# An attention and expert layer on one core: tile 0 is loaded turned, its mean is taken off by products, and its q is made ahead of k and v

## The reference, cut to what matters

```python
def _layernorm(x, axis=-1, eps=1e-05):
    m = jnp.mean(x, axis=axis, keepdims=True)
    v = jnp.var(x, axis=axis, keepdims=True)
    return (x - m) / jnp.sqrt(v + eps)
...
        q = jnp.einsum('bse,ef->bsf', query, Wq)
        k = jnp.einsum('bse,ef->bsf', key, Wk)
        v = jnp.einsum('bse,ef->bsf', value, Wv)
        q = q * cos + _rotate_half(q) * sin
        k = k * cos + _rotate_half(k) * sin
        probs = jax.nn.softmax(jnp.einsum('bhqd,bhkd->bhqk', q, k) * scale, axis=-1)
        ctx = jnp.einsum('bhqk,bhkd->bhqd', probs, v)
        return jnp.einsum('bsf,fe->bse', ctx, Wo)
...
    x = x + xattn(_layernorm(x), ctx_4096, ctx_4096, positions, Wq, Wk, Wv, Wo)
    x = x + ffn(_layernorm(x), A_w, B_w, Wq_w, keys)
```

## Time and profile before

| | before |
|---|---|
| median of 3 runs | 166.45 us (166.23 to 168.49) |
| the profiled execution | 166.19 us |
| its span | 163.6 us |
| outside the span | 2.6 us |
| busy, share of the span | PE 97%, PEld 79%, DVE 83%, ACT 58%, POOL 55% |
| mean granted TensorE clock | 1.000 |
| DMA | 18.45 MB, 113 GB/s on average |
| the chain that ended last | PE 95%, DVE 2%, issue 1% |

### The profile page before, as it was taken

How to read it: one execution, slowest core, us unless ns; L and a number is a source line. 1 busy time by engine, 2 the same in 40 slices (tenths; PEclk the granted TensorE clock), 3 DMA queues, 4 the chain that set the end, 5 groups by cost and what they waited for, 6 DMA issues and landing times.

```text
span 163.6 us, 4199 instructions
## 1 busy us (share of the span) xinstructions
PE 158.4 (97%) x1437; PEld 128.7 (79%) x1437; DVE 135.8 (83%) x394; ACT 95.5 (58%) x215; POOL 89.6 (55%) x115
## 2 busy tenths in 40 slices
PE   6799999999999999999999999999999999999993
PEld 2557886777889787979787987979799986789883
DVE  1979896997998999799888998799886997868562
ACT  3598999899675463933678238832478064414210
POOL 6389999999969944625932098106360305220300
PEclk9999999999999999999999999999999999999999
DMA  5999961403312283434623342133410001000013
GB/s 162 356 411 393 409 221 68 134 31 98 92 48 50 79 251 97 116 112 100 166 85 94 81 105 56 50 98 87 107 62 23 4 0 55 11 6 0 0 64 128
DMA packets 12116, 18.45 MB, mean 113 GB/s; under 512 B 2496, under 2 KB 5056, under 8 KB 11840
## 3 DMA queue, kind: packets, MB, share of 16 engines
q1 hardware_dynamic: 10944, 16.36, 31.7%
q10 hardware_dynamic: 1152, 1.84, 3.7%
HBM read 11.11 MB, written 2.10 MB: 81 GB/s over the span
## 4 chain that ended last, share of the span: by engine, by line
PE 95%; DVE 2%; issue 1%; ACT 0%
PE ps_w L1365 14%; PE ps_w L1370 13%; PE ps_w L1366 12%; PE ps_t L1378 8%; PE ps_w L1358 4%; PE ps_s L1451 4%; PE ps_w L1360 3%; PE ps_w L1359 3%; PE ps_s L1470 3%; PE ps_s L1521 3%; PE ps_t L1521 3%; PE ps_s L1491 2%; PE ps_s L1504 2%; PE ps_t L1370 2%; PE ps_t L1366 2%; PE ps_t L1365 2%
## 5 line engine op out<-in xcount | busy, mean ns | idle before, releaser
L476 POOL TENSOR_TENSOR late<-late,gate 128x512 f32<-128x512 f32 x7 | 7.6, 1087 | 34.3 <-DVE gate L1147 19.3
L707 ACT ACTIVATE eT<-ps_s 128x512 f32<-128x512 f32 x32 | 17.1, 602 | 1.7 <-PE ps_s L1491 0.9
L461 POOL TENSOR_TENSOR oT_lo<-o_n,oT_hi 128x512 fp32r<-128x512 f32 x8 | 10.4, 1296 | 5.3 <-ACT oT_hi L715 5.3
L1365 PE MATMUL ps_w<-am_hi,x2T_hi 128*128 128x288 f32 x44 | 12.6, 308 | 0.0
L1366 PE MATMUL ps_w<-am_lo,x2T_hi 128*128 128x288 f32 x44 | 12.0, 295 | 0.0
L1365 PE MATMUL ps_w<-b_hi,zT_hi 128*128 128x512 f32 (+1 forms) x28 | 11.1, 402 | 0.0
L759 ACT ACTIVATE zT_hi<-ps_t 128x512 fp32r<-128x512 f32 x7 | 4.2, 598 | 11.7 <-PE ps_t L1378 11.7
L1358 PE MATMUL ps_w<-wq_hi,xT_hi 128*128 128x512 f32 x26 | 10.9, 418 | 0.0
L1038 DVE TENSOR_REDUCE ps_s<-ps_s 128x8 f32<-128x512 f32 x16 | 10.6, 688 | 0.3 <-PE ps_s L1451 0.2
L1048 DVE TENSOR_REDUCE ps_s<-ps_s 128x8 f32<-128x512 f32 x16 | 10.4, 691 | 0.5 <-PE ps_s L1470 0.3
L406 POOL TENSOR_TENSOR rstd<-ve,neg_half 128x1 f32<-128x1 f32 x8 | 4.4, 554 | 11.5 <-DVE ve L966 10.2
(11 more groups left out here) (283 smaller groups left out, 551.7 us busy)
## 6 DMA issues: line engine op xcount, KB each, us to landing
x_sb<-x SPq DMA_DIRECT2D x8, 256.0 KB, 6.4
q_stack<-qT_hi SPq DMA_DIRECT2D x32, 64.0 KB, 2.0
cT_in<-cT SPq DMA_DIRECT2D x6, 256.0 KB, 4.1
wq_sb<-wq SPq DMA_DIRECT2D x4, 256.0 KB, 4.4
late<-wo SPq DMA_DIRECT2D x1, 1024.0 KB, 7.2
am_sb<-aT SPq DMA_DIRECT2D x1, 1024.0 KB, 8.9
b_sb<-bT SPq DMA_DIRECT2D x1, 1024.0 KB, 7.3
k_stack<-k_bd_hi SPq DMA_DIRECT2D x32, 32.0 KB, 1.9
```

What stands on the lines that cost most here:

```text
L461: pool.tensor_tensor(oT_lo[:], o_n[:].rearrange("p (b r q) -> p r b q", b=2, r=REP), oT_hi[:].bitcast(F32), ALU.subtract).then_inc(oT_lo_o ...
L707: act.activation(eT[:, c].rearrange("p b n -> p (b n)"), ps_s[:, c, :], ACT.Exp)\
L1365: pe.matmul(dst, hi(k), w_hi[:, k, cols], start=(k == 0), stop=False)
```

## The change

Seven edits, all in the first part of the program.

1. `xT[0]` (tile 0 with the features on partitions) is loaded straight into `xT_raw`. The loads are issued in the order xT[0], wq 0, wq 1, x[0], wq 2, wq 3, x[1], c[0], wkv 0, wkv 1, c[1]; before it was x[0], c[0], wkv 0, wkv 1, wq 0 to 3, x[1], c[1].
2. PE multiplies a tile of 1/512 (`share`) with the four chunks of `xT_raw`, which gives each token's mean on all partitions, and DVE subtracts it from `xT_raw` in place. `turn_xh(0)`, the DVE normalisation and the ACT copy of tile 0 are gone.
3. The scale 1/sqrt(var) of tile 0 goes into its angle table (`cs_0`). Its statistics move on DVE behind the angle steps and just before those of tile 1.
4. PE makes q of tile 0 first, then k and v of tile 0; `turn_k(0)` and `raw_kv(1)` move behind `turn_q(0)` and the route products.
5. ACT splits wq 0 to 2 first, wq 3 behind `normalise(1)`, and wkv only behind the route copy. POOL splits wq 0 and 1 as soon as the mean is off (`x_raw_ok`), no longer behind `rope_step` 9; the four low parts of wkv are all on POOL now, behind `k_blocks(0, ·)`. DVE's share of them (L952) is gone.
6. `pick`, `pick_sum` and `sel` are made at the start.
7. `rotate_k(0)`, `x_low(1)`, `k_low(0)`, `q_low(0)`, `rotate_k(1)` follow each other on DVE behind `q_r`; before, `rotate_k(0)` stood ahead of it, and `k_low(0)` within it.

```diff
+            sp.dma_start(xT_raw[:], xT[0]).then_inc(ld_xT[0], 16)
+            for k in range(2):
+                sp.dma_start(wq_sb[:, k, :], wq[k]).then_inc(ld_wq[k], 16)
             load_x(0)
+            for k in range(2, DK):
+                sp.dma_start(wq_sb[:, k, :], wq[k]).then_inc(ld_wq[k], 16)
+            load_x(1)
             load_c(0)
             for half in range(2):
...
-            for k in range(DK):
-                sp.dma_start(wq_sb[:, k, :], wq[k]).then_inc(ld_wq[k], 16)
-            load_x(1)
             load_c(1)
...
             def first():
+                pool.wait_ge(x_raw_ok, 1)
+                for k in range(2):
+                    split_lo(wq_lo, wq_sb, wq_hi, wq_h, wq_l, k)
                 deviation1(0)
-                pool.wait_ge(rope_step, 9)
-                for k in range(2):
-                    split_lo(wkv_lo, wkv_sb, wkv_hi, wkv_h, wkv_l, k)
-                split_lo(wq_lo, wq_sb, wq_hi, wq_h, wq_l, 0)
-                split_lo(wkv_lo, wkv_sb, wkv_hi, wkv_h, wkv_l, 2)
                 deviation1(1)
-                split_lo(wq_lo, wq_sb, wq_hi, wq_h, wq_l, 1)
+                for k in range(2, DK):
+                    split_lo(wq_lo, wq_sb, wq_hi, wq_h, wq_l, k)
                 k_blocks(0, 0)
                 k_blocks(0, 1)
-                split_lo(wq_lo, wq_sb, wq_hi, wq_h, wq_l, 2)
-                split_lo(wq_lo, wq_sb, wq_hi, wq_h, wq_l, 3)
+                for k in range(3):
+                    split_lo(wkv_lo, wkv_sb, wkv_hi, wkv_h, wkv_l, k)
                 deviation1(2)
+                split_lo(wkv_lo, wkv_sb, wkv_hi, wkv_h, wkv_l, 3)
                 c_low(2)
...
                 normalise(1)
-                act.wait_ge(ld_wq[2], 16)
-                split_hi(wq_hi, wq_sb, wq_h, 2)
-                x_high(1)
-                q_high(0)
                 act.wait_ge(ld_wq[3], 16)
                 split_hi(wq_hi, wq_sb, wq_h, 3)
+                x_high(1)
+                values_out(0)
+                k_high(0)
+                q_high(0)
                 act.wait_ge(route_ps, 1)
                 act.activation(am_sb[:, :, 0:E], ROUTE, ACT.Copy).then_inc(route_ok, 1)
+                for k in range(DK):
+                    act.wait_ge(ld_wkv[k // 2], 16)
+                    split_hi(wkv_hi, wkv_sb, wkv_h, k)
                 value_blocks(0)
...
                 dve.memset(warm[:], 0.0).then_inc(warm_ok, 1)
+                dve.memset(share, 1.0 / D).then_inc(share_ok, 1)
...
                 dve.tensor_scalar(turns[:], ang[:], float(1 / TWO_PI), MAGIC, ALU.mult, ALU.add)\
                    .then_inc(rope_step, 1)
+                dve.wait_ge(xhT_ps, 1)
+                dve.tensor_tensor(xT_raw[:], xT_raw[:],
+                                  xhT_bank(0)[:, 0:P].unsqueeze(1).broadcast_to([P, DK, P]), ALU.subtract)\
+                   .then_inc(x_raw_ok, 1)
                 dve.wait_ge(rope_step, 3)
                 dve.tensor_scalar(turns[:], turns[:], MAGIC, None, ALU.subtract).then_inc(rope_step, 1)
...
-                split_lo(wkv_lo, wkv_sb, wkv_hi, wkv_h, wkv_l_late, 3)
-                dve.wait_ge(cs_ok, 4)
-                rotate_k(0)
+                statistics1(0)
                 statistics1(1)
-                dve.wait_ge(q_ps, 1)
                 H = REP * KVH
                 w = ps_w0[:].rearrange("p (h s j) -> p h s j", h=H, s=2)
+                dve.wait_ge(rstd1_ok, 1)
+                dve.wait_ge(cs_ok, 4)
+                dve.tensor_scalar(cs_0[:], cs[:, 0, :], rstd0[:], None, ALU.mult).then_inc(cs_0_ok, 1)
+                dve.wait_ge(q_ps, 1)
...
                 pe.wait_ge(warm_ok, 1)
                 keep_warm(ps_t1[:], WARM)
-                pe.wait_ge(ident_ok, 1)
-                pe.wait_ge(ld_wkv[0], 16)
-                raw_kv(0, [0, 1])
-                turn_xh(0)
-                pe.wait_ge(ld_wkv[1], 16)
-                raw_kv(0, [2, 3]).then_inc(kv_ps, 1)
+                pe.wait_ge(share_ok, 1)
+                pe.wait_ge(ld_xT[0], 16)
+                for k in range(DK):
+                    mm = pe.matmul(xhT_bank(0)[:, 0:P], share, xT_raw[:, k, :], start=(k == 0), stop=(k == DK - 1))
+                mm.then_inc(xhT_ps, 1)
                 for k in range(DK):
                     pe.wait_ge(ld_wq[k], 16)
                     mm = raw_q(0, k)
                 mm.then_inc(q_ps, 1)
-                turn_k(0)
-                raw_kv(1).then_inc(kv_ps, 1)
-                pe.wait_ge(kT_lo_ok, 1)
+                pe.wait_ge(ld_wkv[0], 16)
+                raw_kv(0, [0, 1])
+                pe.wait_ge(ld_wkv[1], 16)
+                raw_kv(0, [2, 3]).then_inc(kv_ps, 1)
+                pe.wait_ge(ident_ok, 1)
                 turn_xh(1)
                 turn_q(0)
...
                 mm.then_inc(route_ps, 1)
+                turn_k(0)
+                raw_kv(1).then_inc(kv_ps, 1)
                 q_high_part(1, [0, 1])
```

More of the change, by code:

```diff
@@ L241, in build @@
         ld_wq = [sem(f"ld_wq{k}") for k in range(DK)]
-        ld_xT = {t: sem(f"ld_xT{t}") for t in range(DIRECT, T)}
+        ld_xT = {t: sem(f"ld_xT{t}") for t in (0, *range(DIRECT, T))}
+        share_ok, cs_0_ok = sem("share_ok"), sem("cs_0_ok")
         ld_wkv = [sem(f"ld_wkv{half}") for half in range(2)]
@@ L250, in build @@
         rope_step, cs_ok = sem("rope_step"), sem("cs_ok")
-        wq_h, wq_l, wkv_h, wkv_l, wkv_l_late = (sem(n) for n in ("wq_h", "wq_l", "wkv_h", "wkv_l", "wkv_l_late"))
+        wq_h, wq_l, wkv_h, wkv_l = (sem(n) for n in ("wq_h", "wq_l", "wkv_h", "wkv_l"))
         wo_h, wo_l, am_h, am_l, b_h, b_l = (sem(n) for n in ("wo_h", "wo_l", "am_h", "am_l", "b_h", "b_l"))
@@ L487, in _ @@
             pool.memset(neg_half[:], -0.5).then_inc(const_ok, 1)
+            pool.wait_ge(pick_ok, 1)
+            pool.affine_select(out=pick[:], in_=pick[:], compare_op=ALU.not_equal, fill=1.0, base=0,
+                               pattern=[[-(QUAD + 2), PAIRS], [-2 * KVH, 2], [-KVH, 2], [-1, 2]],
+                               channel_multiplier=1).then_inc(pick_ok, 1)
             pool.wait_ge(mask_step, 2)
@@ L760, in z_high @@
                    .then_inc(zT_hi_ok, 1)
[L762 to L767, removed]
             def first():
@@ L771, in first @@
                 act.activation(preload[:, 0:1], half_pi[:], ACT.Sin)
[L772 to L775, removed]
+                for k in range(3):
+                    act.wait_ge(ld_wq[k], 16)
+                    split_hi(wq_hi, wq_sb, wq_h, k)
                 act.wait_ge(rope_step, 9)
@@ L958, in statistics1 @@
                 dve.wait_ge(stat1, 3 * t + 1)
+                if t >= 1:
+                    dve.wait_ge(rstd1_ok, t)
                 if t >= 2:
                     dve.wait_ge(shift1_ok, min(t, DIRECT) - 1)
-                    dve.wait_ge(rstd1_ok, t)
-                else:
-                    dve.wait_ge(xh_ok, 1)
                 dve.bn_aggr(mv1[:], bn1[:]).then_inc(stat1, 1)
@@ L975, in table, with table_0 @@
                     .broadcast_to([P, n, 2, J])
+            def table_0(at, n):
+                return cs_0[:, at:at + HD].rearrange("p (s j) -> p s j", s=2).unsqueeze(1).broadcast_to([P, n, 2, J])
             def table_q(at, t, n):
@@ L1190, in first @@
                 dve.memset(warm[:], 0.0).then_inc(warm_ok, 1)
-                dve.wait_ge(ld_x[0], 16)
-                dve.bn_stats(bn1[:], x_sb[:, 0, :]).then_inc(stat1, 1)
-                dve.wait_ge(stat1, 1)
-                dve.bn_aggr(mv1[:], bn1[:]).then_inc(stat1, 1)
-                dve.wait_ge(stat1, 2)
-                dve.tensor_scalar_add(ve1[:], mv1[:, 1:2], EPS).then_inc(stat1, 1)
+                dve.memset(share, 1.0 / D).then_inc(share_ok, 1)
+                dve.wait_ge(pick_ok, 2)
+                dve.reduce_sum(pick_sum[:], pick[:].rearrange("p c j b h -> p b h c j"), AX.XY).then_inc(sel_ok, 1)
+                dve.wait_ge(sel_ok, 1)
+                dve.tensor_copy(sel[:].rearrange("p b (h k) -> p b h k", h=2),
+                                pick_sum[:].unsqueeze(3).broadcast_to([P, 2, 2, BATCH])).then_inc(sel_ok, 1)
                 dve.wait_ge(ld_pos, 16)
@@ L1245, in first @@
                                   ALU.add).then_inc(q_r_ok, 1)
+                rotate_k(0)
+                x_low(1)
+                k_low(0)
+                q_low(0)
                 rotate_k(1)
-                x_low(1)
-                q_low(0)
                 statistics1(2)
@@ L1586, in raw_q @@
             def raw_q(t, k):
-                pe.wait_ge(x_raw_ok, t + 1)
+                pe.wait_ge(x_raw_ok, 1)
                 return pe.matmul(ps_w0[:], xT_raw[:, k, :], wq_sb[:, k, :], start=(k == 0), stop=(k == DK - 1))
```

48 lines of the change are left out of this document (19 added, 29 removed).

## The result

The change made the kernel slower: 170.28 us in the median of four runs (168.50 to 170.96), against 166.44 for the kernel before. The ratio is 1.022, with a 95% interval of 1.018 to 1.027. (All ratios here leave out executions in a slower state that the chip shows at times, and the medians do not, so two medians do not divide exactly to the ratio beside them.) The profiled execution took 170.59 and its span 168.9; before it was 166.19 and 163.6. So the loss is 5.3 by the two spans, 4.4 by the two executions and 3.8 by the medians. The difference lies in the execution of before that was profiled: in the 50 runs of that kernel beside the experiments the spans are 163.6 to 167.2, with medians of 164.6 and 164.3, and mostly 1.7 to 1.8 lies around them. No span was shorter than that of the profiled one, and 2.6 lay around it.

The account below looks back on a forecast made before the run. PE bounds the kernel, busy for all 20.00 us of a steady window. First scores 2.2 later plus 0.4 for POOL: span 163.6 + 2.6 = 166.2, with 2.6 around it 168.8, plus 0.26 to the median: 169.0; range 166.9 to 171.0.

Parts of the forecast that it names:

- The exclusion: Tile 0's angle steps: DVE operations with two SBUF inputs blocked by POOL's early wq subtractions, costing 1.95 us on DVE.
- `q_b` 1.98 behind q's end: Tile 0: q ends at 10.2 but `q_b` starts only at 12.2, so q waits 2 us for DVE.
- PE's idle before `turn_xh(1)`: Before tile 1's transposes, PE is idle from 11.85 until 13.95, 2.1 us.
- Transposes to first scores: PE from `turn_xh(1)`: 2.88 as before, plus 1.83 of moved work, less 0.2 of wait; first scores at 18.5.
- The loads: New order of the input loads at the start: all cost nothing, zero.
- The first rival: POOL and DVE do not exclude each other at the angle steps: 167.3 us, chance 22%.
- the three cases that the forecast rested on: Rows of before where a DVE operation ended just behind a POOL one: the 1.31 operation, `wkv_lo`, the copy to `sel`.
- the mean's products: Tile 0's mean on PE: four fp32 products of 128 columns taking 0.87 us, between 0.44 and 1.73.
- the POOL term: POOL's longer list makes `q_r` of tile 1 3.2 later, adding 0.4 us at `turn_q(1)` on PE.
- the clock: Rival: PE's clock falls to 1.2 GHz after the idle stretch, `raw_kv(1)` takes 1.73 more; 170.7 us, chance 15%.
- The rival "the change pays": The earlier q of tile 0 is all that counts and POOL's lag is taken up: 166.0 us, chance 6%.

Follow-up runs that it names:

- the fills: Changed kernel with POOL's two early wq subtractions replaced by five memsets of 128x512, low parts of wq 0 and 1 left out: 166.97 us, ratio 1.004.
- the run with the filler: Changed kernel with nine more unused warm-up products on PE between k and v of tile 0 and the turning of tile 1: 168.57 us, ratio 1.017.

## Why the prediction was right in its mechanism and 1.3 us short

169.0 was forecast and 170.28 measured, within the range and on the right side. By its own steps:

**Right in place and size.** The exclusion: two steps of 1.29 and 1.19 (forecast 1.3 and 1.15), with `turns` through ahead of it; the fills bear out the cause. From the release `x_raw_ok` (7.62) to the end of `abs_r` (11.03) it took 3.41; the forecast had 3.45. `q_b` 1.98 behind q's end (2.0). PE's idle before `turn_xh(1)` 1.96 (2.1). Transposes to first scores, at full clock: 4.73 in the run with the filler (4.5). The loads cost nothing. No part of the loss lies in the steady part. The first rival (no exclusion) is refuted. Of the three cases that the forecast rested on, the copy to `sel` says nothing on two inputs: it has one, and it took 0.76 in the kernel after, where no POOL subtraction ran beside it. The other two stand.

**Mis-sized: the mean's products, and the warm-up ahead of them.** `x_raw_ok` came at 7.62 and not at 6.4. Of this, 0.4 is the start (5.05 for 4.65), since the nine warm-up products took 0.57 longer, and 0.8 the length of the products. I had 1.73 as the upper end and took 0.87, "as the kind of product is the same": and so it is, but the row that I scaled, from 11.70 on, was of PE in full work, and I took the warm-up's 3.45 as a constant. The moment at which the rate rises differs between executions: the mean's products took 1.84, 1.58, 1.39 and, four times, 1.05 in the profiles of the seven kernels that have them at this place. 1.05 is 0.87 and the tail, so the term was right for four of these starts and not for this one.

**Mis-sized, and then covered: the POOL term.** I added 0.4 for POOL's longer list. In the kernel after POOL was later by 5.4 and PE by 5.3, and POOL's `q_r` was ready 0.59 before it was needed: there the term is 0, since PE, held up by the clock, came later than POOL. In the six profiles of its variants, where the clock did not fall, `turn_q(1)` begins 0.05 to 0.06 behind the end of `q_r`, and comes 0.17 to 0.19 later against before than the first scores do (for the angles ahead of the mean: 25.02 less 24.02, against 17.07 less 16.24). So the term is there, and its size is 0.2.

**Wrong in its weight: the clock.** I gave the fall 15%, "under one in three of the cases with the long idle". In three of the four runs of the kernel after the mean clock is 0.99 (169.96 to 170.96), in one 1.00 (168.50). The price was right: 1.7 forecast, 1.7 by the filler. Given the idle stretch, the clock's case (170.7) was the likelier one, three of the four runs against one; the rows of before couldn't settle it. The Trainium skill's rule ("TensorE: Matmul & The Clock Gate", Part 4: transposes don't count as busy time in the same way) spoke for it: by it the stretch from 13.17 to `raw_kv(1)` at 16.81 was nearly empty. The fall came at about 17 us, which agrees; the run with 16 warm-up products had the same stretch and kept 1.00, which the rule alone doesn't tell.

The sum in spans: 166.2 forecast, 168.9 measured. First scores came at 21.55 for 18.5, which is 1.2 (later `x_raw_ok`, passed on whole to the transposes), 1.7 (clock) and 0.2 (transposes to scores); less the 0.4 of POOL behind them that makes 2.7. That the time was missed by 1.3 only is luck and no merit of the sum. It started from the shortest span of that kernel with 2.6 around it, and put the 2.6 on top, where the next execution had 1.7: that makes the miss 1.8 for the profiled execution. The other 0.5 is the step from there to the median, forecast as 0.26 up and measured as 0.31 down.

**The rival "the change pays"** named 166.0 with all costs gone. The version with the angles ahead gave 166.42, equal to the kernel before; its argument, that PE starts tile 0 later than it did (5.61), holds (6.92, forecast 6.55).

What stays open: what decides when the rate rises at the start, and whether the clock falls in the gap. No version that was tried beats the kernel before.

## What to carry to other kernels

Before an engine is let go earlier, ask with what it will run beside: a POOL operation that reads SBUF, 1.2 us long, let one DVE operation of two SBUF inputs through and made 0.23 us into 1.3, and the loss was paid at the end of a chain of short dependent steps. Put the short steps into a wait that exists anyway (here DVE's wait for PE's mean), and start the long POOL work behind them; but follow POOL's list too, since what is queued behind that work is moved with it. And a new idle gap on PE costs more than its length: here a gap of 2 us cost another 1.7 at the lower clock in three of four executions, and useless products in the gap won that back in all six.

## What the runs showed of the hardware that was not expected

- Five fills by POOL, 2.45 us together, lengthened none of the five angle steps beside them (0.22, 0.23, 0.23, 0.20, 0.23), where two subtractions by POOL did each time: 1.29 and 1.19 in the kernel after, 1.29 and 1.19 with the filler, 1.01 and 1.27 in the kernel before with POOL's reads added.
- One row speaks for a fill that does hold a DVE operation of one SBUF input, a copy. From the timeline of the kernel after:

```profile
2.13 0.76 DVE L1196 CAST sel<-pick_sum 128x256 fp32r<-128x256 f32 x1
2.22 0.53 POOL L506 MEMSET v_bd<- 128x512 f32 x1
```

  It ends 0.14 behind the fill; a POOL operation of 0.19 and one of 0.24 lie on either side of that. In the kernel before the same copy took 0.80 and ended 0.15 behind a POOL subtraction. No run has the copy alone, so that a fill holds it is likely and not shown.
- A POOL operation on one column did not hold a DVE operation of two SBUF inputs, though it reads SBUF. In the kernel before, `ang` ran beside POOL's power on one column and took 0.24, against 0.22 in the kernel after, where POOL was idle:

```profile
4.73 0.55 POOL L406 TENSOR_TENSOR rstd<-ve,neg_half 128x1 f32<-128x1 f32 x1 [1.37 <-DVE ve L1196]
4.76 0.24 DVE L1201 TENSOR_TENSOR ang<-pos_f,freq 128x64 f32<-128x64 f32 x1
```

- The clock column is no guide at the start: it reads 1.00 for the window from 3 to 5 us in both kernels, though the same nine products took 3.45 in one and 4.02 in the other. What tells the rate there is the duration of known work.
- The same eight passes for the mean took from 1.05 to 1.84, in seven profiles of kernels that begin them at 4.8 to 6.6. Three of these kernels have the same products up to there and took 4.02 for the warm-up, and yet 1.84, 1.58 and 1.39.
